# A recommender tower on one core: a ring counted in columns, gathers ahead of their step, and a top network of 64-output matmuls

## The chip, the core and the metric

The kernel runs on one core of a Trainium2 chip. The metric is the device time of one execution in microseconds: 619.21 before the change, the median of three runs. All arithmetic is in float32.

## What is computed

1024 rows, each with 32 ids. The embeddings (16 numbers each) go through three layers that multiply every field with every map of the layer before, are summed over the 16 dimensions, joined with 16 dense inputs and sent through a network of 512, 256 and 1 outputs.

```python
def _L0_rec_ref(embeddings, W0, W1, W2):          # B=1024 here, M=32 fields, D=16, 64 maps
    x0 = embeddings
    xk = x0
    outs = []
    for W in (W0, W1, W2):
        xk = jax.nn.relu(jnp.einsum('bmd,bhd,mhk->bkd', x0, xk, W))
        outs.append(jnp.sum(xk, axis=2))
    return jnp.concatenate(outs, axis=1)
e = jnp.stack([tbl_0[ids[:, 0]], ..., tbl_31[ids[:, 31]]], axis=1)
z = _L0_rec_ref(e, L0_rec_W0, L0_rec_W1, L0_rec_W2)
h = jnp.concatenate([z, dense_ctx], axis=1)
h = jnp.maximum(h @ W_top1 + b_top1, 0.0)
h = jnp.maximum(h @ W_top2 + b_top2, 0.0)
y = h @ W_top3
```

## The kernel before

The batch is cut into 17 **steps**: two of 32 rows and fifteen of 64, that is 512 and 1024 columns (`width(s)`, 16 per row). A step has three layers. Layer 0 contracts 4 tiles of products, layers 1 and 2 contract 16 each (`TILES`); a tile has 128 partitions, one for a pair of field and map.

What each engine does, in program order, written out by hand with semaphores:

- **GpSimd** gathers embeddings (`gather`, L317, one DMA per 4 rows: 8 or 16 for a step). The first 48, steps 0 to 3, come before anything else. It also makes the products of the last tiles of layers 1 and 2 (`POOL_OF`: none in steps 0 and 1, 3 and 3 in the others, 5 and 4 in the last two), and after each product come as many gathers for the step after next as `GATHERS_AFTER` says.
- **SyncE** (its DMA queue is SPq) waits for a step's gathers, stores its rows in DRAM (`store_rows`, L252), reads them back as `x0g` (L262), and loads the 16 tiles of the step in eight transfers, two tiles each, every field's row repeated for four partitions (`load_tiles`, L289), into the ring `x0bc` of 24 slots of 1024 columns. A slot is taken again when the products of layer 2 that used it are made (`wait_free`). The half-wide tiles of steps 0 and 1 take whole slots in pairs: each pair starts on its own two slots. Store and `x0g` of the next step come behind the last load of a step; only in step 0 they come earlier (`AHEAD`). The weights of the top network are loaded behind steps 1 to 3 (L304).
- **VectorE** makes the other products, two tiles per instruction (L364), in the order layer 1 of step s, layer 0 of step s+1, layer 2 of step s. The first group of a layer is made in two halves. `prod` is a ring of four groups.
- **TensorE** contracts every product tile with its weights (L546), 64 outputs for each half of the columns, the two halves into partitions 0 to 63 and 64 to 127 of one PSUM bank. A float32 matmul shows as two records in the trace.
- **ScalarE** copies a layer's result from PSUM (L446 for VectorE, L463 for GpSimd), applies the ReLU, and does the sums of layer 2 (L453).

The **top network** runs on chunks of steps (`CHUNKS`), in five pieces spread over the steps behind the chunk: FIRST_A and FIRST_B (L606, L607; 512 outputs), SECOND_A and SECOND_B (L612; 256 outputs), THIRD (L617; one output, the weights stationary and the rows moving). The last chunk is the last step alone and comes at the end (`last_chunk`). Ahead of the first products TensorE does matmuls that nobody uses (`keep_going`, L560).

## Time and profile before

| | us |
|---|---|
| runs | 617.38, 619.29, 619.21 (median 619.21) |
| the profiled execution | 620.28, its span 618.5 |
| VectorE busy | 554.7 |
| TensorE busy | 576.0 |
| GpSimd busy | 474.4 |
| ScalarE busy | 306.3 |

The span is what the trace shows; the device time has 1.8 us more around it. The mean granted clock of TensorE over the span is 0.996 of 2.4 GHz. In rows of the timeline the columns are start and duration in microseconds, engine, line, operation, output and input tiles, shapes and count; in brackets stands the idle time of the engine before it and what ended that. "PEld" is TensorE's loading of weights.

### The profile page before, as it was taken

The page shows a single profiled execution, that of the slowest core. Times are in us where ns is not written, and L with a number is a line of the kernel's source. Part 1 is how long each engine was busy: PE and PEld are TensorE (multiplying, and loading weights), DVE is VectorE, ACT ScalarE, POOL GpSimd, SP SyncE. Part 2 cuts the span into 40 slices and gives each one's busy share as a digit, 9 for nine tenths or more (in the row PEclk, how much of TensorE's full clock was granted, in tenths as well). Part 3 has the DMA queues.
Part 4 walks back from the last instruction along what each step waited for, and adds up shares of the span by engine and source line. Part 5 has one row for each costly group of instructions (what it writes and reads, how often), then busy time and mean ns, then how long its engine had stood idle before and what let it go on. Part 6 is the DMA issues. An engine that isn't in the chain of part 4 may idle for free.

```text
span 618.5 us, 8088 instructions
## 1 busy us (share of the span) xinstructions
PE 576.0 (93%) x2716; PEld 205.6 (33%) x2716; DVE 554.7 (90%) x345; ACT 306.3 (50%) x1355; POOL 474.4 (77%) x358
## 2 busy tenths in 40 slices
PE   0899789989999999999999999989999999999997
PEld 0344222323323333333333333333333333333354
DVE  0299899999999999999999999989999999989590
ACT  0133436363547647363555746453565736454442
POOL 6777168979888887889888887988878897949360
PEclk9999999999999999999999999999999999999998
DMA  3777888586776867487876767587775757577000
GB/s 100 238 266 249 324 286 326 207 342 245 310 276 237 289 250 287 154 317 276 314 275 225 304 206 286 195 310 276 285 301 200 306 193 310 218 305 272 1 1 0
DMA packets 35940, 150.89 MB, mean 244 GB/s; under 512 B 7958, under 2 KB 15706, under 8 KB 20538
## 3 DMA queue, kind: packets, MB, share of 16 engines
q1 hardware_dynamic: 27696, 148.26, 63.2%
q0 software_dynamic: 8192, 2.11, 3.0%
q8 instruction: 21, 0.34, 0.2%
q14 instruction: 21, 0.17, 0.1%
q10 hardware_dynamic: 10, 0.00, 0.0%
HBM read 147.20 MB, written 3.15 MB: 243 GB/s over the span
## 4 chain that ended last, share of the span: by engine, by line
DVE 38%; PE 25%; DMA 18%; issue 11%; POOL 4%; SPq 2%; ACT 1%; DVEq 0%; POOLq 0%
DVE prod L364 36%; PE y_ps L546 21%; DMA x0bc<-x_rows 13%; DMA x_rows<-emb 3%; POOL emb L317 3%; DVE z L392 2%; DMA emb<-table,row_sb 2%; POOL pool_prod L332 2%; PE y_ps L560 1%; PE x0g_ps L612 1%; SPq L289 1%; SPq L304 1%; PE x0g_ps L635 0%; SPq L252 0%; PE x0g_ps L617 0%
## 5 line engine op out<-in xcount | busy, mean ns | idle before, releaser
L364 DVE TENSOR_TENSOR prod<-x0bc,x_ps 128x2048 f32<-128x2048 f32 (+2 forms) x272 | 464.1, 1775 | 11.5 <-ACT x_ps L446 11.5
L546 PE MATMUL y_ps<-prod,w_sb 128*64 128x512 f32 (+1 forms) x1792 | 389.6, 566 | 12.3 <-DVE prod L364 11.1
L317 POOL DMA_INDIRECT emb<-table,row_sb x256 | 245.0, 957 | 66.3 <-issue 64.1
L332 POOL TENSOR_TENSOR pool_prod<-x0bc,x_sb 128x1024 f32<-128x1024 f32 x96 | 228.4, 2385 | 58.9 <-ACT x_sb L463 37.1
L546 PEld LDWEIGHTS y_ps<-prod,w_sb 128*64 128x64 f32 x1792 | 123.5, 137 | 254.9 <-issue 203.0
L453 ACT ACTIVATE relu<-y_ps 128x16 f32<-128x16 f32 x480 | 79.6, 292 | 120.7 <-PE y_ps L546 120.7
L446 ACT ACTIVATE x_ps<-y_ps 64x512 f32<-64x512 f32 (+1 forms) x136 | 74.1, 545 | 95.0 <-PE y_ps L546 92.2
L364 DVE TENSOR_TENSOR prod<-x0bc,x0g_ps 128x2048 f32<-128x2048 f32 (+1 forms) x34 | 72.9, 2157 | 29.4 <-DMA x0bc<-x_rows 19.1
L546 PE MATMUL y_ps<-pool_prod,w_sb 128*64 128x512 f32 x384 | 98.6, 594 | 0.7 <-POOL pool_prod L332 0.6
L453 ACT ACTIVATION_READ_ACCUMULATOR relu<-y_ps 128x1 f32 x480 | 79.8, 318 | 0.0
L463 ACT ACTIVATE x_sb<-relu 64x512 f32<-64x512 f32 x120 | 75.4, 629 | 3.2
L546 PE MATMUL y_ps<-prod,w0s_sb 128*64 128x512 f32 (+1 forms) x272 | 60.1, 572 | 7.9 <-DVE prod L364 7.7
L546 PEld LDWEIGHTS y_ps<-pool_prod,w_sb 128*64 128x64 f32 x384 | 27.0, 137 | 55.7 <-issue 48.0
L430 ACT ACTIVATE x0g_ps<-x0g 128x1024 f32<-128x1024 f32 (+1 forms) x17 | 16.6, 978 | 57.6 <-DMA x0g<-x_rows 57.5
L546 PEld LDWEIGHTS y_ps<-prod,w0s_sb 128*64 128x64 f32 x272 | 18.7, 136 | 46.8 <-issue 23.9
L392 DVE TENSOR_REDUCE z<-relu 128x32 f32<-128x512 f32 (+1 forms) x35 | 22.6, 646 | 7.4 <-ACT relu L458 7.4
L560 PE MATMUL y_ps<-w_sb 128*64 128x512 f32 x20 | 11.5, 735 | 18.3 <-DMA x_rows<-emb 18.3
L458 ACT ACTIVATE relu<-y_ps 128x512 f32<-128x512 f32 (+1 forms) x35 | 20.1, 573 | 4.6 <-PE y_ps L546 3.7
L546 PE MATMUL y_ps<-squares,wsq_sb 128*64 128x512 f32 (+1 forms) x68 | 17.3, 568 | 0.0
L436 ACT ACTIVATE squares<-x0g 128x1024 f32<-128x1024 f32 (+1 forms) x17 | 16.8, 991 | 0.0
L612 PE MATMUL x0g_ps<-h,wt_sb 128*128 128x256 f32 (+1 forms) x64 | 14.6, 376 | 0.0
L612 PEld LDWEIGHTS x0g_ps<-h,wt_sb 128*128 128x128 f32 x64 | 11.3, 190 | 5.8 <-issue 4.1
(36 smaller groups left out, 80.9 us busy)
## 6 DMA issues: line engine op xcount, KB each, us to landing
x0bc<-x_rows SPq DMA_DIRECT2D x120, 1024.0 KB, 7.3
x0bc<-x_rows SPq DMA_DIRECT2D x16, 512.0 KB, 6.4
...
emb<-table,row_sb POOLq DMA_INDIRECT x256
...
```

The source lines that it names most:

```text
L317: pool.indirect_dma_start(emb[:, turn, DIM * n:DIM * (n + 1)], None, table, bass.IndirectOffsetOnAxis(row_sb[:, at:at + 1], 0)).then_inc(g ...
L332: pool.tensor_tensor(pool_prod[:, n % POOL_RING, 0:width(s)], x0bc[:, tile_columns(s, j)], x[:, 0:width(s)], ALU.mult).then_inc(pool_produ ...
L364: made = dve.tensor_tensor(out, left, right, ALU.mult)
L392: dve.tensor_reduce(z[:, l, FIRST_ROW[s] // 2:FIRST_ROW[s + 1] // 2], relu[:, l, 0:half(s)].rearrange("p (b d) -> p b d", d=DIM), AX_X, AL ...
L436: act.activation(squares[:, 0:width(s)], x0g[:, 0:width(s)], ACT.Square).then_inc(squared, 1)
L446: act.activation(x[MAPS * copy:MAPS * (copy + 1), h, 0:half(s)], ps[MAPS * h:MAPS * (h + 1), 0:half(s)], ACT.Relu).then_inc(spread_done[l], 1)
L453: act.activation(relu[:, l, cols], ps[:, cols], ACT.Relu, accum_out=z[:, l, at:at + 1]).then_inc(relu_done[l], 1)
L458: act.activation(relu[:, l, 0:half(s)], ps[:, 0:half(s)], ACT.Relu).then_inc(relu_done[l], 1)
L463: act.activation(x_sb[MAPS * copy:MAPS * (copy + 1), half(s) * h:half(s) * (h + 1)], relu[MAPS * h:MAPS * (h + 1), l, 0:half(s)], ACT.Copy ...
L546: made = pe.matmul(ps[MAPS * h:MAPS * (h + 1), 0:half(s)], w, moving[:, half(s) * h:half(s) * (h + 1)], start=first, stop=final)
L560: pe.matmul(y_bank(x)[0:MAPS, :], w1_sb[:, 0, :], w2_sb[:, 0:HALF // MAPS, :], start=True, stop=True)
L612: made = pe.matmul(x0g_ps[:, j, 0:n], wt2_sb[:, k, P * j:P * (j + 1)], h1[:, k, 0:n], start=k == 0, stop=k == H1_TILES - 1)
```

## The change

1. **Ring counted in columns** (`RING_COLUMNS`, `first_column`, `moved`, `landed`, `last_in_place`). Tiles follow each other without gaps, so steps 0 and 1 take 16 half slots each. A transfer always has 2048 columns: two tiles, or four in steps 0 and 1.
2. **Gathers ahead.** Gathers are one sequence, taken by count. 32 come first instead of 48; 16 follow in step 1, 18 in step 2 (`MORE_GATHERS`), 16 in each later step. From step 2 on, two gathers of a step are done one step earlier than before.
3. **Shares.** GpSimd takes 3 and 3 tiles in step 1 (before none) and 2 and 3 in step 2 (before 3 and 3).
4. **Top network.** Each matmul of 128 outputs becomes two of 64, one into each half of the partitions (`by_halves`). In the last layer 64 rows are the stationary side and the weight column moves (`third`); the output is a column of up to 128 partitions, so `y_sb` is copied and stored by columns of up to 128 rows, counted by `y_ready`. The weights are loaded behind steps 2 to 4.
5. **Idle matmuls:** 3 and 2 in place of 7 and 3.

```diff
-MOVED = 2
+BLOCK = 2 * PAIR
-SLOTS = 24
+RING_COLUMNS = 24 * PAIR
-POOL_OF = {0: (0, 0), 1: (0, 0), STEPS - 2: (5, 4), STEPS - 1: (5, 4)}
+POOL_OF = {0: (0, 0), 2: (2, 3), STEPS - 2: (5, 4), STEPS - 1: (5, 4)}
-POOL_BEFORE = {0: [], 3: [2, 3, 5], 4: [2, 3, 4, 5], 5: [2, 3, 4, 5, 5]}
+POOL_BEFORE = {0: [], 2: [3, 5], 3: [2, 3, 5], 4: [2, 3, 4, 5], 5: [2, 3, 4, 5, 5]}
+GATHERED_FIRST = 32
 GATHERS_AFTER = {1: [1, 1, 8], 2: [1, 1, 4]}
-GATHERED_FIRST = 4
+MORE_GATHERS = {(1, 1): [0, 0, 6], (1, 2): [0, 0, 10], (2, 1): [0, 11], (2, 2): [1, 1, 5]}
...
+def columns_out(c):
+    return -(-CHUNK_ROWS[c] // P)
+def first_column(s, j):
+    return TILES * DIM * FIRST_ROW[s] + width(s) * j
 def tile_columns(s, j, count=1):
-    lead = j - j % MOVED
-    at = PAIR * ((TILES * s + lead) % SLOTS) + width(s) * (j - lead)
+    at = first_column(s, j) % RING_COLUMNS
     return slice(at, at + width(s) * count)
+def moved(s):
+    return BLOCK // width(s)
+def landed(s, j):
+    return 16 * sum(1 for i in range(s % 2, s + 1, 2) if TILES // moved(i) > j // moved(s))
+def last_in_place(s, j):
+    a = first_column(s, j) - RING_COLUMNS
+    found = [(i, t) for i in range(s + 1) for t in range(TILES)
+             if a < first_column(i, t) + width(i) and first_column(i, t) < a + BLOCK]
+    by_pool = [x for x in found if x[1] in pool_tiles(x[0], 2)]
+    by_vector = [x for x in found if x not in by_pool]
+    return by_vector[-1:], by_pool[-1:]
...
             def load_tiles(s):
-                for j in range(0, TILES + MOVED, MOVED):
+                for j in range(0, TILES + 1, moved(s)):
...
-                    k = TILES * s + j
-                    if k >= SLOTS:
-                        wait_free(*divmod(k - SLOTS, TILES))
+                    wait_free(s, j)
...
+            all_gathers = iter([(s, n) for s in range(STEPS) for n in range(GATHERS_OF[s])])
+            def gather(count):
+                for s, n in islice(all_gathers, count):
+                    turn, at = s % 2, FIRST_ROW[s] // QUART + n
+                    if n == 0 and s >= 2:
+                        pool.wait_ge(scratch_out[turn], 32 * (s // 2))
...
             def output(c, signal, ps):
...
-                act.activation(y_sb[:, 0:n], ps, ACT.Copy).then_inc(mlp_act, 1)
-                act.wait_ge(mlp_act, PIECES_OF_CHUNK * (c + 1))
-                act.dma_start(out[first:first + n, :].rearrange("b o -> o b"), y_sb[:, 0:n]).then_inc(stored, 16)
+                for col in range(columns_out(c)):
+                    rows = min(P, n - P * col)
+                    act.activation(y_sb[0:rows, col:col + 1], ps[0:rows, col:col + 1], ACT.Copy).then_inc(y_ready, 1)
+                act.wait_ge(y_ready, sum(map(columns_out, range(c + 1))))
+                for col in range(columns_out(c)):
+                    rows = min(P, n - P * col)
+                    act.dma_start(out[first + P * col:first + P * col + rows, :], y_sb[0:rows, col:col + 1]
+                                  ).then_inc(stored, 16)
...
+            def by_halves(ps, w, moving, first, final):
+                for h in range(2):
+                    made = pe.matmul(ps[MAPS * h:MAPS * (h + 1)], w[:, MAPS * h:MAPS * (h + 1)], moving, start=first,
+                                     stop=final)
+                return made
+            def third(c, ps):
+                for b in range(0, CHUNK_ROWS[c], MAPS):
+                    half_of = slice(b % P, b % P + MAPS)
+                    for k in range(H2_TILES):
+                        made = pe.matmul(ps[half_of, b // P:b // P + 1], h2[:, k, b:b + MAPS], wt3_sb[:, k:k + 1],
+                                         start=k == 0, stop=k == H2_TILES - 1)
+                return made
...
                     for k in range(H1_TILES):
-                        made = pe.matmul(x0g_ps[:, j, 0:n], wt2_sb[:, k, P * j:P * (j + 1)],
-                                         h1[:, k, 0:n], start=k == 0, stop=k == H1_TILES - 1)
+                        made = by_halves(x0g_ps[:, j, 0:n], wt2_sb[:, k, P * j:P * (j + 1)], h1[:, k, 0:n], k == 0,
+                                         k == H1_TILES - 1)
...
-            keep_going((0, 0), 7)
+            keep_going((0, 0), 3)
             layer0(0)
-            keep_going((0, 1), 3)
+            keep_going((0, 1), 2)
```

How the instructions stand in a row shows it at three places. First GpSimd, from its first gather (`emb<-table`) to the end of step 2's layers. Before:

```order
L317 DMA emb<-table,row_sb 128x16 x48
L332 TENSOR_TENSOR pool_prod<-x0bc,x_sb 128x1024
L317 DMA emb<-table,row_sb 128x16
L332 TENSOR_TENSOR pool_prod<-x0bc,x_sb 128x1024
L317 DMA emb<-table,row_sb 128x16
L332 TENSOR_TENSOR pool_prod<-x0bc,x_sb 128x1024
L317 DMA emb<-table,row_sb 128x16 x8
```

and now:

```order
L354 DMA emb<-table,row_sb 128x16 x32
L368 TENSOR_TENSOR pool_prod<-x0bc,x_sb 128x512 x3
L354 DMA emb<-table,row_sb 128x16 x6
L368 TENSOR_TENSOR pool_prod<-x0bc,x_sb 128x512 x3
L354 DMA emb<-table,row_sb 128x16 x10
L368 TENSOR_TENSOR pool_prod<-x0bc,x_sb 128x1024 x2
L354 DMA emb<-table,row_sb 128x16 x11
```

Sixteen gathers, those of step 3, have moved behind the products of step 1: six behind layer 1's, ten behind layer 2's.

Second SyncE, steps 1 and 2 (`x_rows<-emb` is a store, in two pieces; what a row waits for stands in brackets). Before:

```order
L289 DMA x0bc<-x_rows 128x1x1024 x4
L289 DMA x0bc<-x_rows 128x1x1024 [waits products] x4
L252 DMA x_rows<-emb 128x256 [waits gathered0]
L252 DMA x_rows<-emb 64x256
L262 DMA x0g<-x_rows 128x1x1024 [waits squared,x0g_placed,scratch_out0]
L304 DMA wt1a_sb<-wt_a 128x512
L289 DMA x0bc<-x_rows 128x1x2048 [waits products] x8
```

and now:

```order
L324 DMA x0bc<-x_rows 128x1x2048 x4
L291 DMA x_rows<-emb 128x256 [waits gathered0]
L291 DMA x_rows<-emb 64x256
L301 DMA x0g<-x_rows 128x1x1024 [waits squared,x0g_placed,scratch_out0]
L324 DMA x0bc<-x_rows 128x1x2048 x4
L324 DMA x0bc<-x_rows 128x1x2048 [waits products] x4
```

Step 1's loads wait for no product, half of step 2's neither, and the weights have moved one step on.

Third TensorE in layer 2 of step 15, around the second and third pieces of a chunk (`h` and `wt_sb` are the hidden layer and the top weights). Before:

```order
L612 MATMUL x0g_ps<-h,wt_sb 128x256 x8
L546 MATMUL y_ps<-prod,w_sb 64x512 x8
L546 MATMUL y_ps<-pool_prod,w_sb 64x512 x2
L546 MATMUL y_ps<-prod,w_sb 64x512 x4
L546 MATMUL y_ps<-pool_prod,w_sb 64x512 x2
L546 MATMUL y_ps<-prod,w_sb 64x512 x4
L617 MATMUL x0g_ps<-h,wt_sb 1x256 x2
```

and now:

```order
L641 MATMUL x0g_ps<-h,wt_sb 64x256 x16
L588 MATMUL y_ps<-prod,w_sb 64x512 x8
L588 MATMUL y_ps<-pool_prod,w_sb 64x512 x2
L588 MATMUL y_ps<-prod,w_sb 64x512 x4
L588 MATMUL y_ps<-pool_prod,w_sb 64x512 x2
L588 MATMUL y_ps<-prod,w_sb 64x512 x4
L650 MATMUL x0g_ps<-wt_sb,h 64x1 x8
```

The places stay; 8 matmuls of 128 outputs are 16 of 64, and two of one output and 256 columns are eight of 64 outputs and one column.

## Rows read from the trace of the kernel before

**Rows 1.** The page: busy time, and the costliest groups of instructions.

```profile
PE 576.0 (93%) x2716; PEld 205.6 (33%) x2716; DVE 554.7 (90%) x345; ACT 306.3 (50%) x1355; POOL 474.4 (77%) x358
...
L546 PEld LDWEIGHTS y_ps<-prod,w_sb 128*64 128x64 f32 x1792 | 123.5, 137 | 254.9 <-issue 203.0
```

**Rows 2.** VectorE's timeline, the start: layer 0 of steps 2, 3; layer 1.

```profile
63.39 2.29 DVE L364 TENSOR_TENSOR prod<-x0bc,x0g_ps 128x2048 f32<-128x2048 f32 x1 [2.83 <-issue]
...
92.84 2.29 DVE L364 TENSOR_TENSOR prod<-x0bc,x0g_ps 128x2048 f32<-128x2048 f32 x1 [0.27 <-issue]
...
113.35 14.46 DVE L364 TENSOR_TENSOR prod<-x0bc,x_ps 128x1024 f32<-128x1024 f32 x8
```

**Rows 3.** VectorE's timeline, steps 4 to 6, 11 and 15.

```profile
148.79 14.46 DVE L364 TENSOR_TENSOR prod<-x0bc,x_ps 128x1024 f32<-128x1024 f32 x8
...
183.13 14.46 DVE L364 TENSOR_TENSOR prod<-x0bc,x_ps 128x1024 f32<-128x1024 f32 x8
198.56 2.29 DVE L364 TENSOR_TENSOR prod<-x0bc,x0g_ps 128x2048 f32<-128x2048 f32 x1 [0.97 <-issue]
201.21 2.29 DVE L364 TENSOR_TENSOR prod<-x0bc,x0g_ps 128x2048 f32<-128x2048 f32 x1 [0.37 <-DMA x0bc<-x_rows]
...
218.99 14.45 DVE L364 TENSOR_TENSOR prod<-x0bc,x_ps 128x1024 f32<-128x1024 f32 x8
...
409.73 2.29 DVE L364 TENSOR_TENSOR prod<-x0bc,x0g_ps 128x2048 f32<-128x2048 f32 x1 [1.83 <-issue]
...
534.17 12.26 DVE L364 TENSOR_TENSOR prod<-x0bc,x_ps 128x1024 f32<-128x1024 f32 x7
```

**Rows 4.** The chain of waits in step 5: start, duration, what.

```profile
184.73 2.52 DMA emb<-table,row_sb
...
187.64 1.96 DMA x_rows<-emb
...
190.83 10.36 DMA x0bc<-x_rows
```

**Rows 5.** GpSimd's timeline: layer 2 of steps 4 and 5, a gather between.

```profile
171.34 2.37 POOL L332 TENSOR_TENSOR pool_prod<-x0bc,x_sb 128x1024 f32<-128x1024 f32 x1 [1.71 <-ACT x_sb L463]
...
182.23 0.94 POOL L317 DMA_INDIRECT emb<-table,row_sb  x1 [0.30 <-issue]
...
205.68 2.37 POOL L332 TENSOR_TENSOR pool_prod<-x0bc,x_sb 128x1024 f32<-128x1024 f32 x1 [0.62 <-ACT x_sb L463]
```

**Rows 6.** The timeline of the first 30 us.

```profile
18.30 8.35 PE L560 MATMUL y_ps<-w_sb 128*64 128x512 f32 x13 [18.30 <-DMA x_rows<-emb]
...
19.18 0.23 PEld L560 LDWEIGHTS y_ps<-w_sb 128*64 128x64 f32 x1 [0.62 <-issue]
...
20.04 0.23 PEld L560 LDWEIGHTS y_ps<-w_sb 128*64 128x64 f32 x1 [0.62 <-issue]
...
23.77 1.22 DVE L364 TENSOR_TENSOR prod<-x0bc,x0g_ps 128x1024 f32<-128x1024 f32 x1 [14.94 <-DMA x0bc<-x_rows]
...
26.03 1.22 DVE L364 TENSOR_TENSOR prod<-x0bc,x0g_ps 128x1024 f32<-128x1024 f32 x1 [1.03 <-DMA x0bc<-x_rows]
...
29.29 1.50 ACT L446 ACTIVATE x_ps<-y_ps 64x256 f32<-64x256 f32 x4 [7.09 <-PE y_ps L546]
```

**Rows 7.** The chain of waits ahead of step 2's layer 0.

```profile
55.78 10.34 DMA x0bc<-x_rows
```

**Rows 8.** The chain of waits, from step 15 to the end.

```profile
538.76 16.53 PE y_ps L546 x76
555.29 3.65 PE x0g_ps L612 x16
...
567.68 0.95 PE x0g_ps L617 x4
...
612.99 2.79 PE x0g_ps L635 x16
...
616.79 0.21 ACT y_sb L499
```

More of the change, by code:

```diff
@@ L1 @@
 from contextlib import ExitStack
+from itertools import islice
 import concourse.bass as bass
@@ L131 @@
 SIGNALS_OF_CHUNK = 5
-PIECES_OF_CHUNK = H1_TILES + H2_TILES + 1
+PIECES_OF_CHUNK = H1_TILES + H2_TILES
 def taken_before(s):
-    return sum(2 if piece in (FIRST_A, FIRST_B) else 1 for i in range(s) for _, piece in PIECES.get(i, []))
+    return sum(2 if piece in (FIRST_A, FIRST_B) else 1 for i in range(s) for _, piece in PIECES.get(i, [])
+               if piece != THIRD)
 def summed2_after(s):
@@ L333, in layer @@
                                        x[:, 0:width(s)], ALU.mult).then_inc(pool_products, 1)
-                    if GATHERED_FIRST <= s + 2 < STEPS:
-                        gather(s + 2, done, done + gathers[k])
-                        done += gathers[k]
+                    if k < len(gathers):
+                        gather(gathers[k])
             pool.wait_ge(ids_in, 32)
@@ L342, in _ @@
             pool.wait_ge(rows_done, 1)
-            gather(0, 0, GATHERS_OF[0])
+            gather(GATHERS_OF[0])
             pool.wait_ge(rows_done, 2)
-            for s in range(1, GATHERED_FIRST):
-                gather(s, 0, GATHERS_OF[s])
+            gather(GATHERED_FIRST - GATHERS_OF[0])
             pool.wait_ge(w0_ready, 2)
@@ L376, in layer @@
                     if l == 1:
[L377 removed]
+                        dve.wait_ge(bc_in[s % 2][group[0] // moved(s)], landed(s, group[0]))
                     n = before((s, l)) + g
@@ L511, in take @@
                 else:
-                    output(c, piece + 1, x0g_ps[0:1, 1, 0:n])
+                    output(c, piece + 1, x0g_ps[:, 1, :])
             def last_chunk():
@@ L601, in mlp @@
                         if c > 0:
-                            pe.wait_ge(mlp_act, PIECES_OF_CHUNK * c)
+                            pe.wait_ge(y_ready, sum(map(columns_out, range(c))))
                     for j in range(2):
-                        ps = x0g_ps[:, piece, CHUNK_B * j:CHUNK_B * j + n]
-                        out_f = slice(P * (2 * piece + j), P * (2 * piece + j + 1))
-                        pe.matmul(ps, wt1a_sb[:, out_f], zt_a[:, 0:n], start=True, stop=False)
-                        made = pe.matmul(ps, wt1b_sb[:, out_f], zt_b[:, first:first + n], start=False, stop=True)
+                        ps, at = x0g_ps[:, piece, CHUNK_B * j:CHUNK_B * j + n], P * (2 * piece + j)
+                        by_halves(ps, wt1a_sb[:, at:at + P], zt_a[:, 0:n], True, False)
+                        made = by_halves(ps, wt1b_sb[:, at:at + P], zt_b[:, first:first + n], False, True)
                 elif piece in (SECOND_A, SECOND_B):
@@ L611, in mlp @@
                     for k in range(H1_TILES):
-                        made = pe.matmul(x0g_ps[:, j, 0:n], wt2_sb[:, k, P * j:P * (j + 1)],
-                                         h1[:, k, 0:n], start=k == 0, stop=k == H1_TILES - 1)
+                        made = by_halves(x0g_ps[:, j, 0:n], wt2_sb[:, k, P * j:P * (j + 1)], h1[:, k, 0:n], k == 0,
+                                         k == H1_TILES - 1)
                 else:
                     pe.wait_ge(mlp_act, PIECES_OF_CHUNK * c + H1_TILES + H2_TILES)
-                    for k in range(H2_TILES):
-                        made = pe.matmul(x0g_ps[0:1, 1, 0:n], wt3_sb[:, k:k + 1], h2[:, k, 0:n], start=k == 0,
-                                         stop=k == H2_TILES - 1)
+                    made = third(c, x0g_ps[:, 1, :])
                 made.then_inc(mlp_mm, 1)
@@ L634, in last_chunk @@
                     for k in range(H1_TILES):
[L635 to L636 removed]
+                        made = by_halves(final_ps[j][:, 0:n], wt2_sb[:, k, P * j:P * (j + 1)], h1[:, k, 0:n], k == 0,
+                                         k == H1_TILES - 1)
                     made.then_inc(mlp_mm, 1)
                 pe.wait_ge(mlp_act, PIECES_OF_CHUNK * FINAL + H1_TILES + H2_TILES)
[L639 to L642 removed]
+                third(FINAL, final_ps[2]).then_inc(mlp_mm, 1)
             pe.wait_ge(weights_in, 16 * 5)
```

68 lines of the change are left out of this document (29 added, 39 removed).

## The prediction

> **What bounds the kernel now.** I read the busy shares of the page first, then VectorE's timeline, then the chain of waits where VectorE stops, then GpSimd's timeline, and last the chain at the end of the span. The shares alone don't decide: TensorE is busy 93% and VectorE 90% [rows 1]. VectorE's timeline does. From layer 1 of step 4 to layer 1 of step 5 it runs without a gap and needs 34.34 us (148.79 to 183.13); the next step takes 35.86 us (to 218.99), and the surplus is a stop before the first product of step 6's layer 0 (0.97 us) and one behind it [rows 3]. Such stops come in every second step; the longest is 1.83 us [rows 3]. Layer 1 of step 3 starts at 113.35 and layer 1 of step 15 at 534.17 [rows 2, 3], so 12 steps take 420.8 us, where 12 x 34.34 would be 412.1: **8.7 us of stops**. The chain of waits says what ends them: the last gather of step 6 goes out at 184.73 and lands 2.52 us later, SyncE at once stores the rows (1.96 us to landing), and then come the loads, the second pair of tiles 10.4 us after the issue [rows 4]. So in the middle the pace is set by GpSimd's last gather, not arithmetic. From 538.8 us on it is different: the chain runs on TensorE almost without a break until the last layer of step 16 [rows 8]. So the time is made of a start (to 113 us), twelve steps, and a TensorE tail.
>
> **The twelve steps: gathers ahead.** The orders show each step keeping its 16 gathers, but two of the next step's are already done, so the last one that a store waits for is the second of the last four instead of the fourth. These two stand at 182.23 and 184.73 [rows 4, 5]: the store, x0g and the loads start **2.5 us earlier**. The stops to be covered are 0.97 plus about 0.4 behind it, at worst 1.83 plus 0.3; the head start is larger than each, by 0.4 to 1.5 us. What is late next is then nothing on DMA's side. GpSimd: its products of layer 2 start at 171.34 and 205.68, 34.34 us apart, of which it waited 0.62 for ScalarE's copy [rows 5], so its own work is 33.7 us, unchanged, and fits under 34.34. TensorE: 76 matmul records take 16.53 us [rows 8], 0.2175 each, so the 148 of a step take 32.2 us and a top-network piece of 8 (half of the 3.65 us of 16 [rows 8]) 1.8 more: 34.0, just under 34.34. The two early gathers wait for the store that last read their buffer; in the step shown it would be the one that landed at 187.64 + 1.96 = 189.6 [rows 4], and they stand some 28 us behind it. Behind that wait stand GpSimd's next products, and it costs nothing. The twelve steps: 12 x 34.34, **-8.7**, with -5.5 as the weak end, if a few tenths stay in most steps and one long stop does.
>
> **The start.** (a) The first load now brings four tiles in one transfer of the same bytes per second. Before, tiles 0 and 1 were in at 23.77 and tiles 2 and 3 at 26.03, each followed by 1.22 us of product [rows 6]. Now both products run from 26.0 to 28.4 instead of ending at 27.25. TensorE was late there, since its idle matmuls ran from 18.30 for 8.35 us [rows 6], and ScalarE got layer 0 only at 29.29; their weight loads follow each other in 0.86 us (19.18, 20.04), twice the 0.43 of a pair of main records, so at the 1.2 GHz level; 3 in place of 7, two records each, are over after 5.2 us. Then TensorE waits for VectorE, and ends some 0.9 us after 28.4. That is **+0.1**. If the gap in TensorE's work lets the granted clock fall to 1.2 GHz again, those matmuls take twice their 0.9: +1.0. (b) The same four-tile load before layer 0 of step 1: estimate +0.5, between 0 and +1. (c) Step 1 gives GpSimd 3 tiles of each layer. A tile of 512 columns is half of the 1.22 us of a pair, so 3 x 0.6, **-1.7** for each of two layers; step 2's layer 1 takes one tile back, +1.1. (d) SyncE's loads of step 1 wait for no product any more, and the loads of step 2 come before they are needed: the stop of 2.83 us before layer 0 of step 2 [rows 2] goes. By (a) to (d) VectorE would be 6 us ahead at step 2.
>
> But the same edit puts a **new wait** in the way. Of step 3's 16 gathers ten now stand behind GpSimd's products of layer 2 of step 1, whose input is ready only when TensorE and ScalarE are through with layer 1. VectorE ended that layer at 63.39 - 2.83 = 60.56 [rows 2]; now at 60.6 + 0.6 - 1.7 = 59.4. In full steps GpSimd starts 8.1 us after VectorE's end (148.79 + 14.46 to 171.34 [rows 3, 5]); with half-width copies I take 4.5 (4.0 to 6.0). Three products of half width (2.37 / 2 each [rows 5]) 3.7, nine gathers at 1.25 = 11.3, the landing of the last 2.5: 81.4. Store and its landing 2.3, x0g and the top weights 1.2: loads at 84.9. The second pair came 10.4 us after its issue, in step 2 as in step 6 [rows 4, 7], the first some 2.6 earlier, so layer 0 of step 3 starts at about 93.2, and it was 92.84 before [rows 2]. VectorE, ready at 59.4 + 28.3 = 87.7 (4.5 layer 0, 7.5 and 15.5 the two layers, 0.8 sums), **waits some 5 us there and gives back all it had won**. The start: **+0.4** (-1.5 to +3). Only the chain through step 1 counts here, so what is won or lost at layer 0 of step 2 is hidden.
>
> **The end.** Tail, TensorE-bound: the pieces with 128 outputs take 3.65 us for 16 records of 256 columns [rows 8], 0.228 each, where two halves of 256 columns side by side should take 0.2175 (a pair of 512 takes twice that); with the seams at both sides I take -0.3 (0 to -0.6) for each of the two double pieces in the tail, and the single ones are under other work. The last layer of a 256-row chunk was 4 records in 0.95 us [rows 8]; now 16 records, each with 64 weight columns and one moving column. The nearest row is 16 records of 128 weight columns with 64 moving ones in 2.79 us, 0.174 each [rows 8]; at half the weights I take 0.087, so 1.4 us (0.9 to 2.8): +0.3 after the seams, and +0.1 for the 192-row chunk. Last chunk: 16 records of 64 columns in 2.79 us become pairs, -1.1 (-0.5 to -1.5); the closing transfer has 64 pieces of 4 bytes in place of one of 256. Before, all that stood behind the last copy (616.79) was 1.7 us [rows 8]; I take +0.5 (0 to 1.1). Copies of one column and the second output transfer of a chunk lie beside other work on ScalarE. The end: -0.6 + 0.4 - 1.1 + 0.5, with 0.1 for an earlier first signal: **-0.9** (-2.6 to +2).
>
> The Trainium skill (TensorEngine Tiling, section Instruction Overhead) speaks against the new last layer: a matmul with one moving column has the same latency as one with 60. By that the 16 records cost like the 64-column row, 2.8 us, and the two chunks of the tail +2.9 in place of +0.4. No row here has one moving column.
>
> **Sum.** +0.4 - 8.7 - 0.9 = -9.2. The profiled execution took 620.28 us (span 618.5), 1.1 above the median of 619.21; I put the change on the median: **610.0 us**, and a profile of about 611.
>
> **Rivals.**
> *The start costs more or the margins don't hold*: the cold clock, a slower GpSimd chain in step 1, or stops of a few tenths left in some steps. For it: the margins of 0.4 to 1.5 us; against: GpSimd's start 8.1 us behind VectorE is very regular. 612 to 617 us.
> *The change doesn't do what it says*, the stops stay, since something other than the last gather sets the loads: 619.2 + 0.4 - 0.9 = 618.7. Against: store and gather follow one another without a gap [rows 4].
> *TensorE becomes the bound (slower)*: the halves don't run side by side in the top network. A piece of 256 columns then takes 3.5 us for 1.8, a step 35.7; ten steps with a piece cost 1.4 each over 34.34, and the tail 7 more: 619.2 + 0.4 - 8.7 + 14 + 7 - 0.9 = 631. It turns slower than before from a piece of about 2.9 us. Against it: two halves are how the 76 records of 64 outputs reach 0.2175 each, which is half of what 512 columns cost one alone. The Trainium skill (TensorE: Matmul & The Clock Gate, section What overlaps and what doesn't, under Part 3) says that a weight load overlaps a running matmul only when the row group differs, and here both halves use all rows; by that a pair would pay for its weights too. The profile has 137 ns for a load of 64 columns [rows 1], so 8 pairs would pay 1.1 us, which lies at the point where the change turns. The records of the main layers, all rows in both halves as well, don't pay it.
>
> **Chances.** Forecast, 606 to 612: 0.68. Start or margins worse: 0.20. No effect: 0.07. TensorE-bound: 0.03. Better than 606: 0.02. The range takes in the bounds of start, stops and tail: 605.5 to 615. A measurement of this kernel tells about 0.3% (1.9 us): faster by more 0.90, within 0.07, slower 0.03.
>
> **What would show it.** Right: VectorE has no stop before layer 0 from step 4 to 16 and 34.3 us per step; a stop of about 5 us before layer 0 of step 3, ended by a load whose chain goes back to GpSimd's gathers of step 1; layer 1 of step 3 at 113 to 115 us and of step 15 near 526. The last layer at about 1.4 us. Wrong: stops that remain with the gathers landed long before, TensorE behind by more than 4 us in steps with a piece, or layer 0 of step 3 later than 96 us.

## The result: slower, by stores in pieces of 4 bytes

The changed kernel takes **625.02 us** (median, 624.44 to 625.31); the kernel before, beside it, 619.16. The ratio is 1.010, interval 1.008 to 1.0121. Forecast were 610.0 us and the range 605.5 to 615.0: wrong sign, far outside. The profiled execution took 625.31 us, its span is 623.4. Page of the changed kernel, beside [rows 1]; VectorE's timeline at (s,1), the start of layer 1 of step s, beside [rows 2, 3]:

```profile
span 623.4 us, 8499 instructions
PE 563.9 (90%) x2910; PEld 205.8 (33%) x2910; DVE 552.2 (89%) x343; ACT 308.7 (50%) x1367; POOL 478.8 (77%) x363
...
q10 hardware_dynamic: 1168, 0.00, 0.1%
...
93.82 2.29 DVE L398 TENSOR_TENSOR prod<-x0bc,x0g_ps 128x2048 f32<-128x2048 f32 x1 [5.49 <-DMA x0bc<-x_rows]
...
114.53 14.46 DVE L398 TENSOR_TENSOR prod<-x0bc,x_ps 128x1024 f32<-128x1024 f32 x8
...
338.74 2.29 DVE L398 TENSOR_TENSOR prod<-x0bc,x0g_ps 128x2048 f32<-128x2048 f32 x1 [2.31 <-issue]
...
462.37 13.32 DVE L398 TENSOR_TENSOR prod<-x0bc,x_ps 128x1024 f32<-128x1024 f32 x7
478.81 1.22 DVE L398 TENSOR_TENSOR prod<-x0bc,x_ps 128x1024 f32<-128x1024 f32 x1 [3.12 <-PE y_ps L588]
481.58 4.49 DVE L398 TENSOR_TENSOR prod<-x0bc,x0g_ps 128x2048 f32<-128x2048 f32 x2 [1.55 <-PE y_ps L588]
...
502.87 1.21 DVE L398 TENSOR_TENSOR prod<-x0bc,x_ps 128x1024 f32<-128x1024 f32 x1
...
537.22 2.34 DVE L398 TENSOR_TENSOR prod<-x0bc,x_ps 128x1024 f32<-128x1024 f32 x2
```

TensorE and VectorE are busy for 12.1 and 2.5 us less than before [rows 1], GpSimd and ScalarE for 4.4 and 2.4 us more; what grew is the waiting. Queue q10 is ScalarE's, the output: 1168 packets. The span cut at four points, for all kernels whose start is comparable ("tail": (15,1) to the issue of the last output transfer; "last transfer": from there to the end of the span):

| kernel | us, ratio to before [interval] | (3,1) | twelve steps | tail | last transfer |
|---|---|---|---|---|---|
| before | 619.16 | 113.35 | 420.8 | 82.9 | 1.5 |
| changed | 625.02, 1.010 | 114.53 | 422.7 | 79.4 | 6.8 |
| row_output_2 | 612.36, 0.9929 [0.9901, 0.9957] | 114.79 | 413.1 | 80.2 | 1.5 |
| row_one_ahead | 611.31, 0.9907 [0.9875, 0.9938] | 113.15 | 414.5 | 80.2 | 1.5 |
| row_no_halves | 616.13, 0.9987 [0.9956, 1.0017] | 113.75 | 414.1 | 83.0 | 1.5 |
| column_alone_2 | 626.91, 1.0179 [1.0129, 1.0228] | 112.84 | 421.4 | 81.0 | 6.8 |
| middle_outputs_out | 616.27, 0.9977 [0.9951, 1.0004] | 114.94 | 412.3 | 80.2 | 6.7 |
| quads | 614.19, 0.9937 [0.9913, 0.9961] | 114.60 | 415.6 | 81.7 | 1.7 |
| pairs (one run) | 619.49, beside 619.84 | 115.04 | 417.8 | 80.5 | 3.7 |
| columns_one_ahead | 621.53, 1.0055 [1.0026, 1.0084] | 113.53 | 420.7 | 79.1 | 7.1 |
| row_behind_product | **609.46, 0.9858** [0.9831, 0.9885] | 113.22 | 412.2 | 80.4 | 1.5 |
| before_burst | 617.53, 0.9998 [0.9971, 1.0025] | 116.30 | 416.9 | 82.1 | 1.5 |
| ahead_alone | 613.15, 0.9922 [0.9894, 0.9949] | 111.37 | 414.1 | 82.1 | 1.5 |
| ahead_and_halves | 610.89, 0.9909 [0.9876, 0.9941] | 112.72 | 413.9 | 80.2 | 1.5 |

The kernel before took 616.83 to 617.90 (medians) beside the others, so ratios compare better than times; the four points are read from one trace of each kernel. Before to changed, in spans: start +1.2, steps +1.9, tail -3.5, last transfer +5.3, together +4.9. Seven steps do take 34.35 us (3, 4, 5, 10 to 12 and 14), as forecast. Step 9 takes 37.4 (321.96 to 359.33) and step 13 takes 40.5 (462.37 to 502.87). Both begin just after a chunk's output goes out (at 319.8 and 460.2 us). The other two such outputs (571.2 and 606.1) fall into the tail, where TensorE sets the pace. In step 12, from the timeline (GpSimd, ScalarE's queue, SyncE's queue):

```profile
460.21 1.29 ACTq L542 DMA_DIRECT2D out<-y_sb  x2
...
461.47 0.94 POOL L354 DMA_INDIRECT emb<-table,row_sb  x1 [0.30 <-issue]
462.72 0.95 POOL L354 DMA_INDIRECT emb<-table,row_sb  x1 [0.30 <-issue]
469.93 0.94 POOL L354 DMA_INDIRECT emb<-table,row_sb  x1 [6.26 <-issue]
...
468.14 1.36 SPq L291 DMA_DIRECT2D x_rows<-emb  x2
```

The gather issued at 461.47 is the last that the store of step 14's rows waits for. That store goes out 6.7 us later; in row_output_2 it is 2.5 (457.82 to 460.29). Ahead of step 9's long wait it is the same: 7.4 us (321.02 to 328.42), in row_output_2 2.4 (321.00 to 323.38). And in step 12 GpSimd itself stands still for 6.3 us before its next gather.

### The profile page after: what moved, and what is told of

Read it like the earlier page. It is cut to its first block, busy times and chain, and to the rows that moved or that the text cites. A ratio compares the mean times of both kernels' runs of the same rounds, so it can differ in the third digit from the quotient of the medians.

```text
span 623.4 us, 8499 instructions
## 1 busy us (share of the span) xinstructions
PE 563.9 (90%) x2910; PEld 205.8 (33%) x2910; DVE 552.2 (89%) x343; ACT 308.7 (50%) x1367; POOL 478.8 (77%) x363
## 3 DMA queue, kind: packets, MB, share of 16 engines
q10 hardware_dynamic: 1168, 0.00, 0.1%
## 4 chain that ended last, share of the span: by engine, by line
PE 30%; DVE 23%; POOL 19%; DMA 15%; issue 11%; ACT 1%; SPq 1%; DVEq 0%; POOLq 0%
PE y_ps L588 28%; DVE prod L398 22%; POOL emb L354 11%; DMA x0bc<-x_rows 10%; POOL pool_prod L368 8%; PE x0g_ps L641 2%; DMA emb<-table,row_sb 2%; DMA x_rows<-emb 1%; DMA x0g<-x_rows 1%; DVE z L426 1%; ACT x_ps L482 1%; DMA off_sb<-id_offset 0%; SPq L324 0%; SPq L301 0%; SPq L291 0%
## 5 line engine op out<-in xcount | busy, mean ns | idle before, releaser
L368 POOL TENSOR_TENSOR pool_prod<-x0bc,x_sb 128x1024 f32<-128x1024 f32 (+1 forms) x101 | 233.2, 2316 | 48.2 <-ACT x_sb L499 40.3
L588 PEld LDWEIGHTS y_ps<-prod,w_sb 128*64 128x64 f32 x1772 | 127.3, 137 | 246.3 <-issue 197.2
L588 PE MATMUL y_ps<-pool_prod,w_sb 128*64 128x512 f32 (+1 forms) x404 | 103.1, 588 | 9.2 <-POOL pool_prod L368 9.0
L499 ACT ACTIVATE x_sb<-relu 64x512 f32<-64x512 f32 (+1 forms) x128 | 78.8, 615 | 3.4
L489 ACT ACTIVATION_READ_ACCUMULATOR relu<-y_ps 128x1 f32 x480 | 79.4, 317 | 0.1
L588 PEld LDWEIGHTS y_ps<-pool_prod,w_sb 128*64 128x64 f32 x404 | 29.3, 138 | 65.2 <-issue 39.4
L602 PE MATMUL y_ps<-w_sb 128*64 128x512 f32 x10 | 6.4, 781 | 18.1 <-DMA x_rows<-emb 18.1
L641 PE MATMUL x0g_ps<-h,wt_sb 128*64 128x256 f32 (+2 forms) x160 | 15.1, 338 | 0.7 <-ACT h L523 0.7
L641 PEld LDWEIGHTS x0g_ps<-h,wt_sb 128*64 128x64 f32 x160 | 10.2, 137 | 7.3 <-issue 3.1
```

The source lines that it names most:

```text
L368: pool.tensor_tensor(pool_prod[:, n % POOL_RING, 0:width(s)], x0bc[:, tile_columns(s, j)], x[:, 0:width(s)], ALU.mult).then_inc(pool_produ ...
L489: act.activation(relu[:, l, cols], ps[:, cols], ACT.Relu, accum_out=z[:, l, at:at + 1]).then_inc(relu_done[l], 1)
L499: act.activation(x_sb[MAPS * copy:MAPS * (copy + 1), half(s) * h:half(s) * (h + 1)], relu[MAPS * h:MAPS * (h + 1), l, 0:half(s)], ACT.Copy ...
L588: made = pe.matmul(ps[MAPS * h:MAPS * (h + 1), 0:half(s)], w, moving[:, half(s) * h:half(s) * (h + 1)], start=first, stop=final)
L641: made = pe.matmul(ps[MAPS * h:MAPS * (h + 1)], w[:, MAPS * h:MAPS * (h + 1)], moving, start=first, stop=final)
```

## Experiments

Six runs (row_output, two_gathers_back, row_and_back, column_alone; store_late, before_burst_of_six) were made where the kernel before itself took 659.5 and 656.6 us. Their traces begin late (VectorE's first product of layer 1 starts at 47.9 us in row_output and at 72.6 in column_alone, 29.3 in row_output_2 and 30.1 in the kernel before), and I haven't followed why. Their ratios to the kernel before beside them were 0.958 (row_output), 0.980 (two_gathers_back), 0.964 (row_and_back) and 1.018 (column_alone); store_late and before_burst_of_six ran once each, at 635.8 and 660.3 us. I use only their steps and stops, and no times.

### The output as before: row_output, row_output_2

```diff
-    return -(-CHUNK_ROWS[c] // P)
+    return 1
-        y_sb = sb("y_sb", [P, CHUNK_B // P])
+        y_sb = sb("y_sb", [1, CHUNK_B])
...
-                        made = pe.matmul(ps[half_of, b // P:b // P + 1], h2[:, k, b:b + MAPS], wt3_sb[:, k:k + 1],
+                    made = pe.matmul(ps[0:1, 0:n], wt3_sb[:, k:k + 1], h2[:, k, 0:n], start=k == 0,
...
+                act.dma_start(out[first:first + n, :].rearrange("b o -> o b"), y_sb[:, 0:n]).then_inc(stored, 16)
```

> The changed kernel with its last layer and its output as before: the column wt3_sb stationary, 64 to 256 rows moving, y_sb one partition wide, one transfer per chunk in place of two. Everything else of the change stays. Theory A (the transfers out of y_sb by columns, 4 bytes from each of up to 128 partitions, cost the time: some 5.3 us at the very end, where the last one takes from 616.62 to 623.4 and took from 617.03 to 618.5 before, and the long steps 9 and 13, because the gathers in flight beside them land late): 625.0 - 5.3 - 2.4 (step 9) - 5 (step 13) = 612.3 us, 610.5 to 614.5; steps 9 and 13 within 0.5 of 34.5. Theory B (the gathers ahead are what makes the long steps, through GpSimd's stop before gather 114 and 226; the outputs cost at the end alone): 625.0 - 5.3 = 619.7, step 13 stays near 40. Theory C (the top network by halves disturbs TensorE): 619.7 or more, with stops elsewhere.

> The kernel of row_output once more, since in its first run the kernel before itself took 659.5 us on that chip and the weights landed late. There its steps 9 and 13 were 34.34 us each, and steps 7 and 14 began 35.4 and 35.2 after the ones before them. Theory A, now with GpSimd's stop as a second cost of its own (0.8 to 1.1 us at gather 114 and at gather 226): (3,1) to (15,1) in 12 x 34.34 + 2.2 = 414.3 us, the end 5.3 us shorter than in the changed kernel, together 625.0 - (422.7 - 414.3) - 5.3 = 611.3, 610.3 to 612.5. Theory B (GpSimd's stop alone makes the long step 13): 619.

612.36 us, steps 9 and 13 at 34.35 and 34.53, the last transfer 1.5 us: theory A. (In row_output's own trace step 9 takes 34.3 us and step 13 35.2, not 34.34 as the text on row_output_2 has it.) VectorE's and GpSimd's timeline of row_output_2, step 13, and the last transfer of both kernels (spans 609.6 and 623.4):

```profile
458.72 14.46 DVE L398 TENSOR_TENSOR prod<-x0bc,x_ps 128x1024 f32<-128x1024 f32 x8
473.10 4.48 DVE L398 TENSOR_TENSOR prod<-x0bc,x0g_ps 128x2048 f32<-128x2048 f32 x2
...
457.82 0.95 POOL L354 DMA_INDIRECT emb<-table,row_sb  x1 [0.31 <-issue]
459.07 0.95 POOL L354 DMA_INDIRECT emb<-table,row_sb  x1 [0.30 <-issue]
462.07 0.94 POOL L354 DMA_INDIRECT emb<-table,row_sb  x1 [2.06 <-issue]
...
608.12 0.21 ACTq L538 DMA_DIRECT2D out<-y_sb  x1
```

```profile
616.62 0.47 ACTq L542 DMA_DIRECT2D out<-y_sb  x1
```

What the small pieces do to the gathers is in the DMA view, by queue (packets, MB, share of 16 engines; q1 is SyncE's, the loads and stores). The changed kernel, 461 to 464 us, then row_output_2, 457 to 461 us:

```profile
q0 software_dynamic: 78, 0.02, 61.5%
q1 hardware_dynamic: 41, 0.20, 16.7%
q10 hardware_dynamic: 279, 0.00, 5.5%
```

```profile
q1 hardware_dynamic: 70, 0.44, 26.9%
q0 software_dynamic: 125, 0.03, 7.5%
q10 hardware_dynamic: 2, 0.00, 0.1%
```

A packet of the gathers' queue q0 takes 0.615 x 3 x 16 / 78 = 0.38 us beside 279 output packets, 0.075 x 4 x 16 / 125 = 0.04 us beside two. SyncE's packets take no longer than without the output (0.20 and 0.25 us each), so the price falls on the gathers. The output's own packets are short (a share of 5.5%, 0.01 us each). At the end of the changed kernel, where one other packet is all that moves, it is the same: the last transfer's 80 packets are busy for 0.4% of 9 us (615 to 624 us) and finished 1.3 us after its issue, yet it lands 6.4 us after it.

```profile
q10 hardware_dynamic: 80, 0.00, 0.4%
...
out<-y_sb ACTq DMA_DIRECT2D x1, 0.2 KB, 6.4
```

So the time passes between the last packet and the landing; what happens there no trace shows.

### The output by columns in the kernel before: column_alone_2

The reverse edit (`third`, `y_sb` and `output` of the change, nothing else); column_alone is the same kernel.

> The kernel of column_alone once more, for the same reason. In its first run the steps 9, 13 and 15 had stops of 3.8 us in VectorE's layer 0, and the end from (16,2) on took some 35 us. Theory A: 619.2 + 5.3 (end) + 3 to 8 (steps 9 and 13) = 627 to 632, 629. Theory B: 624.5. Theory C (columns cost nothing): 619 to 620.

626.91 us, just under theory A's range: the last transfer +5.3, step 9 with a stop of 3.2 us and step 13 with 2.4, at 38.1 and 37.2 us. This part alone costs 1.8%. Its trace, of the fastest of the four runs (623.81), shows only some 3.5 us of that: the twelve steps hardly grow in sum (421.4 for 420.8), since the stops of other steps are fewer here than in the kernel before, and the tail is 1.9 us shorter. Where the slower runs lost the rest stays open.

### Is it the transfers or the matmuls? middle_outputs_out, quads, pairs

```diff
-                for col in range(columns_out(c)):
+                for col in range(columns_out(c) if c == FINAL else 0):
                     rows = min(P, n - P * col)
                     act.dma_start(out[first + P * col:first + P * col + rows, :], y_sb[0:rows, col:col + 1]
```

> The changed kernel with the transfers of y_sb to out left out for the first four chunks (rows 0 to 959 of the output are not stored); their matmuls and ScalarE's copies by columns stay, and so does the last chunk with its transfer. Theory A (the transfers, not the matmuls or copies by columns, delay the gathers beside them): steps 9 and 13 at 34.35 to 34.9, (3,1) to (15,1) as in row_output_2 in 413.1 in place of 422.7, the end unchanged: 625.0 - 9.6 = 615.4, 614.5 to 617. If the matmuls or copies do it: 625.

Beside the transfers the edit takes out ScalarE's wait for the transfer of the chunk before, issued 10 us or more earlier. The twelve steps take 412.3 us in place of 422.7, the end keeps its 6.7: only the transfers do it, and in the steps they cost 10.4 us. GpSimd's stops are still there (1.90 and 1.88 us), and steps 6 and 13 take 34.39. quads:

```diff
-                        made = pe.matmul(ps[half_of, b // P:b // P + 1], h2[:, k, b:b + MAPS], wt3_sb[:, k:k + 1],
+                        made = pe.matmul(ps[0:n // 4, j:j + 1], h2[:, k, j:n:4], wt3_sb[:, k:k + 1],
...
+                act.dma_start(out[first:first + n, :].rearrange("(p j) o -> p (j o)", j=4), y_sb[0:n // 4, :]
```

> The changed kernel with the output still by rows stationary, but each partition holds four neighbouring rows (h2's columns taken with a stride of 4, at most 64 outputs on 64 partitions), so that a chunk is stored in one transfer of 16 bytes from each of 64 partitions (16 at the end) in place of 256 and 64 writes of 4 bytes. Theory D (the price of such a transfer grows with the number of small writes): the last transfer takes 1.5 to 3.5 us from issue to the end of the span in place of 6.8, and steps 9 and 13 lose most of their stops: 625.0 - 4 - 7 = 614, 612.5 to 616. Theory E (any transfer from many partitions in pieces under some size costs its 6 us whatever the number): 622 to 625.

> The kernel of quads with two neighbouring rows per partition in place of four: a chunk is stored in 128 pieces of 8 bytes, the last one in 32. If the price grows evenly with the number of pieces (1.8 us for 16, 6.8 for 64, so 0.10 each): the last transfer takes 3.5 us (3.0 to 4.0) from issue to the end of the span. If it needs pieces of 4 bytes: 1.5 to 2. If anything over 16 pieces pays in full: 6 or more.

quads takes 614.19 us, as expected of theory D. With a chunk of 256 rows stored in 1, 64, 128 and 256 pieces (row_output_2, quads, pairs, changed) step 9 takes 34.35, 34.85, 35.31 and 37.37 us, step 13 34.53, 36.30, 36.95 and 40.50. The tail of quads is 2.3 us longer than the changed kernel's; I haven't followed why. The last transfers of quads (span 613.7) and pairs (span 617.1):

```profile
611.94 0.32 ACTq L538 DMA_DIRECT2D out<-y_sb  x1
```

```profile
613.36 0.32 ACTq L538 DMA_DIRECT2D out<-y_sb  x1
```

256 bytes in 1, 16, 32 and 64 pieces take 1.5, 1.7, 3.7 and 6.8 us to the end of the span: theory D, some 0.1 us for each piece above 16. Whether the number or the size of the pieces counts these runs don't separate, since the bytes are the same. The Trainium skill (DMA: Bandwidth & Descriptors, Specifications) says that below 512 bytes the DMA reads, modifies and writes. All four forms lie below that, and they take from 1.5 to 6.8 us; the threshold alone doesn't tell them apart.

### GpSimd's stop: two_gathers_back, row_and_back, row_one_ahead, columns_one_ahead

Each takes gathers ahead away again, in `MORE_GATHERS`: `(2, 2): [1, 1, 3]` for none ahead, `[1, 1, 4]` for one.

> The changed kernel with two gathers fewer ahead: layer 2 of step 2 issues 3 instead of 5 after its last product, so that from step 3 on every step issues the gathers of before and gather 114 and 226 stand behind a product again. Output by columns as in the change. Theory A: only the slips of steps 6 to 8 go (0.8 + 0.2 + 0.4) and some of step 13, 625.0 - 1.4 to - 3.5 = 622.5 (621 to 624), the last transfer still 6.8 us, step 13 still over 37. Theory B: GpSimd's stops of 2.6 and 6.3 us go, steps 6 to 8 and 13 are 34.4 each, 625.0 - 1.4 - 6 = 617.5, with only step 9 and the end left.

> Both edits: output and last layer as before, two gathers fewer ahead. Both theories: all twelve steps at 34.35, 625.0 - 5.3 - 10.5 (twelve steps 412.2 in place of 422.7) = 609.2, 608 to 611. If it stays above 613, something else of the change (halves, ring) costs what I put down to outputs and gathers.

> Output and last layer as before, and one gather ahead in place of two (layer 2 of step 2 issues 4 after its last product): gathers 114 and 226 then stand behind GpSimd's first product of layer 1, 113 and 225 ahead of it. Theory A with the stop at a fixed count of gathers, waiting for the one just issued: the product hides it, no idle time of over 0.5 us ahead of either, the twelve steps at 34.35 = 412.3, so 2 us less than row_output_2: 609.3, 608.3 to 610.5. If the stop has to do with the steps' own state (a store landing, code being loaded) and not with the count, it stays: 611.3.

> The changed kernel with one gather ahead in place of two, output by columns as in the change. Is step 13 (40.5 us) so long because two causes meet there? Theory A: the transfers alone cost it what they cost in column_alone_2 (37.2 us with two gathers not ahead), GpSimd's stop before gather 226 the rest: step 13 now 37 to 37.5, step 9 37.2, steps 6 to 8 at 34.35, 625.0 - 1.4 - 3.2 = 620.4, 619.4 to 622. If the transfers alone cost 6 us in step 13: 623.6.

With two gathers ahead GpSimd stops 2 to 3 us before gathers 114 and 226 even with the output as before (2.06 in the rows above). With none or one ahead the stop at 114 is gone in all four, and step 6 takes 34.35 to 34.56 us in three of them. But fewer gathers ahead bring VectorE's stops back: row_and_back has five of 0.5 to 1.45 us from step 4 on, and its twelve steps take 417.8 us, where I had expected 412.2. two_gathers_back falls between its two theories: step 13 takes 36.3 us (over 37 or 34.4), step 9 38.1, the twelve 421.9. In row_one_ahead neither stop came, as expected, and still the steps took 414.5 us and not 412.3; the largest part stands at layer 0 of step 4 (0.62 and 0.39 us). That a head start of one gather, 1.25 us, doesn't cover every stop is the likely reason, not a shown one. My 609.3 there was too low. In columns_one_ahead steps 9 and 13 take 37.8 and 37.1 us, near the 37.2 and 37 to 37.5 expected (the sum came out 1 us above), so of step 13's 40.5 in the changed kernel 3.4 come from the two causes meeting. They meet here as well, a little: gather 226 stops for 2.75 us in spite of the product before it, because the gathers land late.

### What the stop waits for: before_burst, before_burst_of_six, store_late

```diff
-GATHERS_AFTER = {1: [1, 1, 8], 2: [1, 1, 4]}
+GATHERS_AFTER = {1: [0, 2, 8], 2: [1, 1, 4]}
```

> The kernel before with one edit: in every step's layer 1 GpSimd issues no gather after its first product and two after its second (one and one before), so gathers 113 and 114, and 225 and 226, stand back to back. If the stop goes by the count: an idle time of 1.9 to 2.6 us on GpSimd ahead of gather 114 and of gather 226, nowhere else, and the products behind it that much later; the time within 1 us of the kernel before, since the gathers of a step still end where they did. If the stop came with the change: no idle time over 0.5 us ahead of any gather.

No stop: 113 and 114 began at 227.09 and 228.38. So GpSimd doesn't wait for the gather just before. Its time is that of the kernel before, ratio 0.9998. In all 15 stops so far the stopped gather begins 1.80 us, within 0.02, after the last landing of gather 112 or 224, which is also when the step's store is issued (468.14 and 469.93 above), since both are the last gather of a step. Next:

```diff
+MORE_GATHERS = {(5, 2): [1, 1, 6], (6, 1): [0, 0, 8], (8, 2): [1, 1, 6], (9, 1): [0, 0, 8]}
```

> The kernel before with one edit: layer 2 of step 5 issues six gathers after its last product in place of four, so that 109 to 114 stand in one burst (layer 1 of step 6 two fewer), and the same two steps of distance later, at gathers 157 to 162 (steps 8 and 9), as a control. If the stop goes by the count of gathers and waits for gather 112's landing: GpSimd idle 1.9 to 2.9 us ahead of gather 114, which begins 1.75 to 1.85 us after the last landing of 112, and no idle time over 0.35 us ahead of 162. If the stop needs something that the change brought: none at either.

```diff
                 sp.wait_ge(gathered[turn], 16 * sum(GATHERS_OF[turn:s + 1:2]))
+                if s == 7:
+                    sp.wait_ge(products, before((6, 1)) + 3)
```

> The kernel of row_output_2 with the store of step 7's rows held back until VectorE's third product of step 6's layer 1, some 4 us later (223.5 to 224.5 in place of 219.67). If GpSimd's stop before gather 114 waits for the landing of gather 112: it still ends 1.75 to 1.85 us after that landing, near 221.45, and lasts 2 to 2.9 us. If it waits for the store: it ends near 225.5 and lasts some 6 us. The time within 1.5 us of row_output_2 in the first case.

GpSimd's timeline in before_burst_of_six, gathers 112 to 114 and 161, 162; and in store_late (gathers 113 and 114, with SyncE's store):

```profile
260.62 0.95 POOL L320 DMA_INDIRECT emb<-table,row_sb  x1 [0.30 <-issue]
261.88 0.94 POOL L320 DMA_INDIRECT emb<-table,row_sb  x1 [0.30 <-issue]
264.69 0.95 POOL L320 DMA_INDIRECT emb<-table,row_sb  x1 [1.88 <-issue]
...
368.89 0.95 POOL L320 DMA_INDIRECT emb<-table,row_sb  x1 [0.30 <-issue]
370.15 0.94 POOL L320 DMA_INDIRECT emb<-table,row_sb  x1 [0.30 <-issue]
```

```profile
238.92 0.95 POOL L356 DMA_INDIRECT emb<-table,row_sb  x1 [0.30 <-issue]
242.98 0.95 POOL L356 DMA_INDIRECT emb<-table,row_sb  x1 [3.11 <-issue]
...
245.41 0.86 SPq L293 DMA_DIRECT2D x_rows<-emb  x2
```

The stop shows in the kernel before as well once its gathers stand in a burst, at 114 and not at 162, which is also the second gather after a step's last; it ends 2.04 us after gather 112's last recorded landing, a little above the 1.85 expected (this trace has only part of the landings). In store_late it lasts 3.11 us, for 2 to 2.9 expected, and ends before the store is issued, 1.8 us after gather 112 landed (241.2 in the landing records). So it is tied to the count of gathers and waits for the gather two before; with 256 gathers only 114 and 226, 112 apart, could be seen. In the kernel before a product stands between, and nothing shows. What in GpSimd's handling of transfers makes it so, these runs don't show.

### The best version: row_behind_product, ahead_alone, ahead_and_halves, row_no_halves

row_behind_product is row_output with gathers 114 and 226 behind a product:

```diff
-MORE_GATHERS = {(1, 1): [0, 0, 6], (1, 2): [0, 0, 10], (2, 1): [0, 11], (2, 2): [1, 1, 5]}
+MORE_GATHERS = {(1, 1): [0, 0, 6], (1, 2): [0, 0, 10], (2, 1): [0, 11], (2, 2): [1, 1, 5],
+                (5, 2): [1, 1, 3], (6, 1): [2, 1, 8], (12, 2): [1, 1, 3], (13, 1): [2, 1, 8]}
```

> Output and last layer as before, two gathers ahead as in the change, but gathers 114 and 226 moved behind GpSimd's next product (layer 2 of steps 5 and 12 issues 3 after its last product, layer 1 of steps 6 and 13 two after its first). Theory: neither stop, twelve steps at 34.35 = 412.2 in place of 413.1, and step 15's layer 0 in time: 612.4 - 1.2 = 611.2, 610.3 to 612; the best of both kernels. Rival (what is late next, GpSimd's products on full tiles, takes it back): 612.4.

```diff
-                for h in range(2):
-                    made = pe.matmul(ps[MAPS * h:MAPS * (h + 1)], w[:, MAPS * h:MAPS * (h + 1)], moving, start=first,
+                return pe.matmul(ps, w, moving, start=first, stop=final)
```

> The kernel of row_output with the top network's matmuls of 128 outputs again (one matmul for the two halves). What is measured is the halves alone. At the end the 16 matmuls of the last chunk's second layer take 2.79 us in place of 1.15, and the 9 late ones of the first layer 0.5 more: row_output_2 + 2.1, 613.4. In the steps TensorE is not the bound, so nothing: the twelve steps equal within 0.3 us. Rival: the longer pieces delay TensorE's last matmuls of a layer, and so VectorE: up to + 3 more.

The kernel before with the change's sequence of gathers (`all_gathers`), 48 first, and

```diff
+MORE_GATHERS = {(2, 2): [1, 1, 6], (5, 2): [1, 1, 3], (6, 1): [2, 1, 8], (12, 2): [1, 1, 3], (13, 1): [2, 1, 8]}
```

> The kernel before with two gathers ahead from layer 2 of step 2 on, and gathers 114 and 226 behind a product as in row_behind_product; ring in tiles, start, top network and output as before. Theory (the steps' stops of 0.55 to 1.84 us went because the last gather of each step is issued some 2.5 us sooner): twelve steps at 34.35 with one stop of up to 0.6 at the first, 412.2 to 413, in place of 420.8, and step 15's stop of 1.8 gone too: 8 + 1.1 less than before, ratio 0.985. Rival (it takes the ring in columns or the early loads as well): stops of 0.5 to 1 us stay in some steps, ratio over 0.990.

> ahead_alone with the top network's matmuls of 64 outputs side by side, last layer and output as before. The end 1.6 to 2 us shorter than in ahead_alone (16 records of 2.53 to 2.79 us against 32 of 1.18, and the 9 late ones 0.5), ratio to ahead_alone 0.997; the steps equal within 0.3 us. About equal to row_behind_product: what the ring in columns and the other start add is then 0 to 1 us.

row_behind_product takes 609.46 us, below the 610.3 to 612 expected: all twelve steps at 34.35, from VectorE's timeline

```profile
113.22 2.34 DVE L399 TENSOR_TENSOR prod<-x0bc,x_ps 128x1024 f32<-128x1024 f32 x2
...
525.37 4.54 DVE L399 TENSOR_TENSOR prod<-x0bc,x_ps 128x1024 f32<-128x1024 f32 x3
```

Two gathers ahead, alone in the kernel before, bring 0.8%: one stop of 1.6 us is left at layer 0 of step 4 and none over 0.3 us behind it in the twelve steps. The ratio, 0.992, is short of the 0.985 expected and on the rival's side of 0.990, though the profile (span 609.0) is where I put it; the other runs were slower (up to 614.7). The stops that the rival wants are not in the trace, and what slowed those runs is open. The halves shorten the tail by 1.9 us (82.1 to 80.2), 2.8 in the other pair (83.0 to 80.2), where I had expected 2.1. Part of the second is the clock: the last chunk's 16 records of 128 outputs take 2.53 us in row_no_halves, at a granted clock of 0.76, and 2.01 in ahead_alone, at 0.99. In row_no_halves the steps grew by 1.0 and the start shrank by 1.0, so its span is 2.7 us longer than row_output_2's; its median is 3.8 longer, 616.1 and not 613.4. ahead_and_halves is 0.996 of ahead_alone, as expected. Its span (608.3) and that of row_behind_product (607.2) leave 1.1 us for the ring in columns and the other start, the medians 1.4; their ratios' intervals overlap, so the size of this rest is not settled.

## Why the prediction was wrong

- **Start: right.** VectorE stops 5.49 us before layer 0 of step 3, at 93.82; forecast were 5 and 93.2. (3,1) came 1.2 us later than before, forecast 0.4.
- **Steps, mechanism: right.** Two gathers ahead take the stops away: 34.35 us in seven steps of the changed kernel, and 412.2 for twelve in row_behind_product, where I had 412.1. ahead_alone shows that the gathers do it and not the ring.
- **"Copies of one column and the second output transfer of a chunk lie beside other work on ScalarE": the step that failed.** True of ScalarE, but I priced a transfer by the engine that issues it, and so put it at nothing. A chunk's 256 pieces (192 in the fourth) delay the gathers in flight beside them, and behind the last gather stands the chain that I had called the pace-setter myself: gather, store, loads [rows 4]. Measured: 10.4 us in the steps, part of it where the late gathers meet GpSimd's stop.
- **"Behind that wait stand GpSimd's next products, and it costs nothing": failed in two steps.** I had checked the wait for the store. The stop at gathers 114 and 226 is another one; alone it costs some 1 us (413.1 and 412.3 with it, 412.2 without), together with the late gathers 3.4 of step 13's 6.2 us too many. There TensorE did 6.47 us of work in 9.7, and in the 7 us behind that its granted clock was 0.51, the 1.2 GHz level: the windows from 462.3 and from 472 us (us, PE, PEld, DVE, ACT, POOL busy, PEclk, DMA share, GB/s):

```profile
462.30:472.00 9.70, 6.47 (x30) 2.11 (x26) 9.70 (x7) 6.72 (x70) 3.11 (x4) 1.00 0.38 28
472.00:479.00 7.00, 5.69 (x14) 1.69 (x16) 3.88 (x3) 2.24 (x3) 6.64 (x5) 0.51 0.94 343
```

- **The closing transfer, +0.5 (0 to 1.1): mis-sized by ten.** It cost 5.3, mostly behind its last packet. I had said that 64 pieces of 4 bytes replace one of 256 bytes, and bounded the price by the 1.7 us that stood behind the last copy before, a row of another form of transfer; no row bounded it from above.
- **Tail: better than forecast**, -3.5 for -1.4. The 32 small records of the last chunk take 1.18 us (2.79 before [rows 8]; -1.6 for -1.1), and the last layer is nearly free. Half of the -1.6 is luck: the row of 2.79 us stood at a granted clock of 0.68, and at full clock the same 16 records take 2.01 us, so the halves themselves bring 0.8. The windows of the 16 records, before and in ahead_alone (columns as above), then TensorE's timeline and chain in the changed kernel:

```profile
612.99:615.78 2.79, 2.78 (x16) 2.59 (x16) 0.00 (x0) 0.31 (x1) 0.00 (x0) 0.68 0.00 0
```

```profile
604.32:606.33 2.01, 2.00 (x16) 1.86 (x16) 0.00 (x0) 0.31 (x1) 0.00 (x0) 0.99 0.00 0
```

```profile
570.28 0.63 PE L650 MATMUL x0g_ps<-wt_sb,h 128*64 128x1 f32 x16
570.71 1.11 PE L588 MATMUL y_ps<-pool_prod,w_sb 128*64 128x512 f32 x4
...
614.24 1.18 PE x0g_ps L641 x32
```

16 records of one moving column (8 matmuls) hold TensorE up for 0.43 us, from 570.28 to 570.71, 0.027 each; I took 1.4. The 2.8 us that I set against it came from my row, 128 weight columns at a clock of 0.68, and not from the rule. The Trainium skill (TensorEngine Tiling, Instruction Overhead) gives each matmul some 60 cycles; at 2.4 GHz that is an estimated 0.4 us for 16 records, and the trace agrees.
- **Rivals.** TensorE did not become the bound: the loads of weights for the 32 small records lie inside their 1.18 us. "Slower" came true by a mechanism that was none of my rivals. Of the start and margins 0.8 us came.
